# Rolling the feed-forward chunk loops of a 12-layer attention + FFN kernel into register loops, with three changes of order inside a chunk

## The chip, the cores and the metric

The kernel runs on one core of a Trainium2 chip. The metric is the device time of one execution in microseconds (us). Five engines work side by side, each from its own instruction stream: TensorE (PE, matmuls; its weight loads are shown apart as PEld), VectorE (DVE), ScalarE (ACT), GpSimd (POOL) and SyncE (SP, which here only issues DMAs). They are tied together by counting semaphores alone.

## The reference

```python
def attn(x, Wqkv, bqkv, Wproj, bproj):          # 12 layers, 16 heads, no softmax
    for i in range(12):
        qkv = x @ Wqkv[i].T + bqkv[i]
        q, k, v = split heads of qkv
        att = einsum('bhqd,bhkd->bhqk', q, k) * scale
        y = einsum('bhqk,bhkd->bhqd', att, v)
        x = y @ Wproj[i].T + bproj[i] + x
    return x

x = layernorm(x + attn(x))                      # x: (16, 256, 128) float32
gate, up = x @ wg.T, x @ wu.T                   # hidden 384, weights are integers / 127
x = layernorm(x + (silu(gate) * up) @ wd.T)
```

## The kernel before

Since the attention has no softmax, the kernel never forms the tokens' activations in the 12 layers. It keeps, for each of the 16 batches, a 128 x 128 matrix that stands for all the layers so far, and one Gram matrix of the input; each layer is a chain of small matrix products on them. This part takes the first 255 us or so and the change does not touch it.

The change is in the last stage, the feed-forward part, which runs over `CHUNKS` = 8 chunks of `CT` = 4 tiles of 128 tokens. What is done for a chunk c, by engine:

- POOL `centre` (line 329) writes the centred input of a chunk into `xc`, of which there are two slots; `rstd1_part` and the first half of `norm2` raise a 128 x 4 variance to the power -1/2 (line 366); `norm2` (line 371) then scales the finished rows into `o`, and SP (line 311) sends each finished chunk out.
- PE `z_stage` (line 910) multiplies `xc` by the batch's matrix into PSUM bank 4; `ht_stage` (line 919) transposes the normalised rows `h1` into bank 5; `gate_stage` (line 925) makes the three gate and three up products, two passes each of 128 x 512; `down_stage` (line 940) multiplies the 384 hidden rows back to 128.
- ACT `norm1` (line 465) scales z into `h1` by four small instructions; `ht_copy` (line 473) takes the upper part of the transposed rows out of PSUM; `gate` (line 477) is the silu of one gate product.
- DVE `z_part` (line 640) takes z out of PSUM; `var1_part` sums its squares; `ht_part` (line 661) makes the lower part `ht_lo`; `hid_part` (line 666) multiplies silu and up product; `y_part` (line 672) adds the residual, and a second `var_part` sums the squares of y.

In the names of the profile `sg` and `hid` are views of `xt`, `o` is `xchan`, `nu_b` is `gram`.

The chunks are software-pipelined: PE's `chunk(c)` (line 975) does the gate stage of chunk c, z of chunk c+2, the transposes of chunk c+1, and then the down stage of chunk c. The order on each engine is that in which its `chunk` function is written, and nothing else sets it. Before the change all eight calls of `chunk` are written out on every engine, with constants in every wait and address. Only PE has a second version of the eight chunks with a third pass, `chunks(True)`, whose first six chunks stand in a loop; it is taken when the lower part of the weights isn't zero. In these inputs it is zero, so that PE runs `chunks(False)` and then jumps over the other version (line 998).

`loop(eng, count)` (line 255) is a loop on one engine's instruction stream with a register as its counter and a hint for the fetch of the jump back. In it a wait for `c + 2` needs a register that holds the sum.

## Time and profile before

| | |
|---|---|
| time, median of 3 runs | 325.33 us (324.76 to 326.08) |
| the profiled execution | 325.33 us, span 323.5 us |
| PE busy | 310.8 us, 96% of the span |
| PE weight loads busy | 291.4 us, 90% |
| DVE busy | 223.2 us, 69% |
| ACT busy | 183.5 us, 57% |
| POOL busy | 95.9 us, 30% |
| mean granted TensorE clock | 0.995 of full speed |

Busy times count engine work only; register, branch and semaphore instructions are not in them. Between the span of the profile and the time of the execution lie 1.8 us. The chunks of the feed-forward part start on PE at 262.70, 269.68, 276.64, 283.60, 290.56, 297.52, 304.48 and 311.45 us, and PE's last matmul is over at about 318 us.

### The profile page before, as it was taken

What the parts mean: (1) busy time and instruction counts of PE and PEld (TensorE: products, weight loads), DVE (VectorE), ACT (ScalarE), POOL (GpSimd) and SP (SyncE); (2) the same over time, 40 slices, a digit from 0 to 9 for tenths busy, and PEclk for the clock granted to TensorE, in tenths of its full rate; (3) what the DMA queues carried; (4) which work ended last, traced back from release to release, by engine and by line L of the source; (5) the groups of instructions that cost most, each with busy time, mean ns of one, the idle gap of its engine ahead of it and who ended that gap; (6) DMA issues with size and microseconds to landing.
All of it is one profiled execution on the core that took longest, in us unless ns stands there. A gap on an engine that the chain in (4) does not pass through costs nothing.

```text
span 323.5 us, 9031 instructions
## 1 busy us (share of the span) xinstructions
PE 310.8 (96%) x3792; PEld 291.4 (90%) x3792; DVE 223.2 (69%) x638; ACT 183.5 (57%) x417; POOL 95.9 (30%) x89
## 2 busy tenths in 40 slices
PE   8999999999999999999999999999999999999993
PEld 8989899899898998989989899898998999998872
DVE  0367776775867757767577676777768568888863
ACT  2438758475583865837748477484672174445540
POOL 2014055050410603206032060230605134555432
PEclk9999999999999999999999999999999999999997
DMA  7842001020020200202002020020000000211112
GB/s 277 321 168 75 6 19 58 2 77 2 2 75 5 75 2 3 75 4 77 0 4 76 2 76 3 2 76 2 2 3 2 3 0 2 65 35 32 32 34 70
DMA packets 7594, 14.94 MB, mean 46 GB/s; under 512 B 512, under 2 KB 4736, under 8 KB 7424
## 3 DMA queue, kind: packets, MB, share of 16 engines
q1 hardware_dynamic: 6976, 13.27, 12.3%
q10 hardware_dynamic: 576, 1.06, 0.9%
q8 instruction: 32, 0.52, 0.7%
q14 instruction: 10, 0.08, 0.1%
HBM read 12.23 MB, written 2.10 MB: 44 GB/s over the span
## 4 chain that ended last, share of the span: by engine, by line
PE 92%; DVE 4%; DMA 1%; issue 1%; ACT 1%; POOLq 0%; POOL 0%
PE ps L835 14%; PE ps L782 13%; PE ps L868 13%; PE ps L734 7%; PE ps L732 7%; PE ps L733 7%; PE ps L947 6%; PE ps L801 4%; PE ps L937 3%; PE ps L936 3%; DVE s_rows L568 3%; PE ps L821 3%; PE ps L750 2%; PE ps L914 2%; PE ps L808 2%; PE ps L793 2%
## 5 line engine op out<-in xcount | busy, mean ns | idle before, releaser
L350 POOL TENSOR_TENSOR step_lo<-step,step_hi 128x512 fp32r<-128x512 f32 x44 | 54.9, 1280 | 172.3 <-ACT step_hi L431 172.3
L732 PE MATMUL ps<-state_hi,step_hi 128*128 128x258 f32 x176 | 50.7, 288 | 0.0
L835 PE MATMUL ps<-s_rows,w 32*128 32x256 f32 x768 | 44.8, 380 | 5.3 <-DVE s_rows L568 5.3
L734 PE MATMUL ps<-state_hi,step_lo 128*128 128x258 f32 x176 | 49.8, 283 | 0.0
L733 PE MATMUL ps<-state_lo,step_hi 128*128 128x258 f32 x176 | 49.6, 282 | 0.0
L835 PEld LDWEIGHTS ps<-s_rows,w 32*128 32x128 f32 x768 | 40.4, 185 | 7.2 <-ACT s_rows L425 7.2
L431 ACT CAST step_hi<-step 128x512 fp32r<-128x512 f32 x44 | 27.0, 619 | 33.7 <-DVE step L574 33.7
L782 PE MATMUL ps<-w,gram 128*128 128x128 f32 x352 | 42.8, 275 | 0.0
L782 PEld LDWEIGHTS ps<-w,gram 128*128 128x128 f32 x352 | 42.0, 192 | 0.6
L868 PE MATMUL ps<-step,gram 128*128 128x128 f32 x320 | 40.6, 281 | 0.0
L868 PEld LDWEIGHTS ps<-step,gram 128*128 128x128 f32 x320 | 37.3, 192 | 3.3 <-DVE step L574 3.3
L609 DVE TENSOR_TENSOR state_lo<-ps,state_hi 128x512 fp32r<-128x512 f32 x44 | 30.5, 692 | 12.2 <-ACT state_hi L435 10.7
L422 ACT COPY gk<-ps 128x512 f32<-128x512 f32 x48 | 28.1, 589 | 18.3 <-PE ps L782 18.3
L449 ACT COPY gram<-ps 128x256 f32<-128x256 f32 x88 | 33.0, 375 | 6.7
L574 DVE TENSOR_TENSOR step<-ps,cst 128x512 f32<-128x512 f32 x48 | 30.9, 686 | 8.3 <-PE ps L835 8.3
L621 DVE TENSOR_TENSOR state_lo<-ps,state_hi 128x256 fp32r<-128x256 f32 x88 | 36.6, 416 | 0.0
L450 ACT CAST state_hi<-ps 128x256 fp32r<-128x256 f32 x88 | 33.6, 382 | 0.0
L733 PEld LDWEIGHTS ps<-state_lo,step_hi 128*128 128x128 f32 x176 | 33.4, 190 | 0.0
L732 PEld LDWEIGHTS ps<-state_hi,step_hi 128*128 128x128 f32 x176 | 33.3, 189 | 0.0
L734 PEld LDWEIGHTS ps<-state_hi,step_lo 128*128 128x128 f32 x176 | 33.2, 189 | 0.0
L435 ACT CAST state_hi<-ps 128x512 fp32r<-128x512 f32 x44 | 25.9, 588 | 6.3 <-PE ps L868 6.3
L617 DVE TENSOR_TENSOR means<-ps,shift 128x4 f32<-128x4 f32 x88 | 14.3, 163 | 18.6 <-ACT state_hi L450 18.5
(102 smaller groups left out, 496.7 us busy)
## 6 DMA issues: line engine op xcount, KB each, us to landing
w<-weights SPq DMA_DIRECT2D x12, 592.5 KB, 3.7
xchan<-x_chan SPq DMA_DIRECT2D x1, 2048.0 KB, 10.6
out<-xchan SPq DMA_DIRECT2D x7, 256.0 KB, 2.5
xt<-x_tok ACTq DMA_DIRECT2D x4, 258.0 KB, 5.5
xt<-x_tok SPq DMA_DIRECT2D x4, 258.0 KB, 5.1
fw_int<-ffn_weights SPq DMA_DIRECT2D x1, 576.0 KB, 4.9
out<-xchan SPq DMA_DIRECT2D x2, 128.0 KB, 2.6
cst<-consts SPq DMA_DIRECT2D x1, 146.5 KB, 7.2
```

What stands on the lines that cost most here:

```text
L350: nc.gpsimd.tensor_tensor(group(step_lo, g), group(step, g), group(step_hi_f, g), ALU.subtract).then_inc(step_lo_ready, 1)
L449: nc.scalar.copy(gram[:, 2 * e:2 * e + 2, :], ps[:, two, 0:P]).then_inc(gram_ready, 1)
L450: nc.scalar.copy(state_hi[:, 2 * e:2 * e + 2, S_B:S_B + P], ps[:, two, P:2 * P]).then_inc(b_hi_ready, 1)
L574: nc.vector.tensor_tensor(group(step, g), n_banks(g // 2)[:, :, P * j:P * (j + 1)], (project if last else ident).unsqueeze(1).to_broadcast ...
L609: nc.vector.tensor_tensor(state_lo[:, GB * g:GB * (g + 1), S_H:S_H + P], products(H_BANKS[g]), state_hi_f[:, GB * g:GB * (g + 1), S_H:S_H ...
L621: nc.vector.tensor_tensor(state_lo[:, 2 * e:2 * e + 2, S_B:S_B + P], ps[:, two, P:2 * P], state_hi_f[:, 2 * e:2 * e + 2, S_B:S_B + P], ALU ...
L732: nc.tensor.matmul(dst, l_hi, r_hi, start=True, stop=False)
L733: nc.tensor.matmul(dst, l_hi, r_lo, start=False, stop=False)
L734: return nc.tensor.matmul(dst, l_lo, r_hi, start=False, stop=True)
L782: last = nc.tensor.matmul(one_product(GK_BANKS[g], b), gram_raw[:, b, 0:P] if first else gram[:, b, :], w[:, s, WK:WK + P], start=True, st ...
L835: last = nc.tensor.matmul(n_banks(h)[:, k, :], w[r, s, WQ + P * i:WQ + P * (i + 1)], s_rows[r, h, i, :], start=i == 0, stop=i == QUADS - 1)
L868: last = nc.tensor.matmul(one_product(H_BANKS[g], b), gram_raw[:, b, 0:P] if first else gram[:, b, :], step[:, b, :], start=True, stop=True)
```

## The change

It does five things.

1. SP, POOL, ACT, DVE and PE run most of their chunks in a register loop of two chunks per pass (one transfer per pass on SP). PE, DVE and ACT make three passes (chunks 0 to 5), POOL two (chunks 0 to 3), SP seven; the remaining chunks stay written out. PE's version with two passes per product, which is the one that runs, is looped too.
2. PE transposes the rows of chunk c+1 (`ht_stage`) ahead of z of chunk c+2 (`z_stage`); it was the other way round.
3. DVE follows: `ht_part(c + 1)` ahead of `z_part(c + 2)`.
4. ACT normalises chunk c+1 (`norm1`) after the first silu of chunk c instead of after the second.
5. POOL's `centre` runs three chunks ahead instead of four and stands ahead of `norm2` instead of behind it; `centre(3, 1)` ahead of the first chunk is gone, since chunk 0 now does it.

```diff
-            for c in range(CHUNKS - 1):
+            with loop(sp, CHUNKS - 1) as c:
                 sp.wait_ge(o_ready, c + 2)
...
-            def chunk(c, slot, ahead=4):
+            def chunk(c, slot, ahead=3):
 
                 if ahead >= 2:
                     pool.wait_ge(h1_ready, (c + 1) * CT + CT)
                     rstd1_part(c + 2)
+                if ahead >= 3:
+                    pool.wait_ge(z_done, c + 2)
+                    centre(c + 3, 1 - slot)
                 if ahead > 0:
                     norm2(c)
-                if ahead >= 4:
-                    pool.wait_ge(z_done, c + 3)
-                    centre(c + 4, slot)
...
-            pool.wait_ge(z_done, 2)
-            centre(3, 1)
-            for c in range(CHUNKS):
+            with loop(pool, CHUNKS // 2 - 2) as i:
+                for s in range(2):
+                    chunk(i * 2 + s, s)
+            for c in range(CHUNKS - 4, CHUNKS):
                 chunk(c, c % 2, CHUNKS - 1 - c)
...
                 gate(c, 0)
-                gate(c, 1)
                 if not last:
                     norm1(c + 1, 1 - slot)
+                gate(c, 1)
                 gate(c, 2)
...
-            for c in range(CHUNKS):
-                chunk(c, c % 2, last=c == CHUNKS - 1)
+            with loop(act, CHUNKS // 2 - 1) as i:
+                for s in range(2):
+                    chunk(i * 2 + s, s)
+            chunk(CHUNKS - 2, 0)
+            chunk(CHUNKS - 1, 1, last=True)
...
                 for j in range(HC):
                     hid_part(c, j)
-                if ahead >= 2:
-                    z_part(c + 2, c + 2, slot)
                 if ahead >= 1:
                     ht_part(c + 1)
                 if ahead >= 2:
+                    z_part(c + 2, c + 2, slot)
...
-            for c in range(CHUNKS):
-                chunk(c, c % 2, CHUNKS - 1 - c)
+            with loop(dve, CHUNKS // 2 - 1) as i:
+                for s in range(2):
+                    chunk(i * 2 + s, s)
+            chunk(CHUNKS - 2, 0, ahead=1)
+            chunk(CHUNKS - 1, 1, ahead=0)
...
+                if ahead >= 1:
+                    ht_stage(c + 1, 1 - slot)
                 if ahead >= 2:
                     pe.wait_ge(z_ready, c + 2)
                     z_stage(c + 2, c + 2, slot)
-                if ahead >= 1:
-                    ht_stage(c + 1, 1 - slot)
                 down_stage(c, last_chunk=ahead == 0)
 
             def chunks(low):
-                if low:
-                    with loop(pe, CHUNKS // 2 - 1) as i:
-                        for s in range(2):
-                            chunk(i * 2 + s, s, low)
-                for c in range(CHUNKS - 2 if low else 0, CHUNKS):
-                    chunk(c, c % 2, low, CHUNKS - 1 - c)
+                with loop(pe, CHUNKS // 2 - 1) as i:
+                    for s in range(2):
+                        chunk(i * 2 + s, s, low)
+                chunk(CHUNKS - 2, 0, low, ahead=1)
+                chunk(CHUNKS - 1, 1, low, ahead=0)
```

PE, the end of chunk 0 before the change: after the last gate product come z (L914, `ps<-a_cent,xc`), the transposes (L922, `ps<-cst,h`), and the down products (L947).

```order
L936 MATMUL ps<-ht_hi,wgu_hi 128x512 [waits silu_ready]
L937 MATMUL ps<-ht_lo,wgu_hi 128x512
L914 MATMUL ps<-a_cent,xc 128x128 [waits xc_ready,z_ready]
L914 MATMUL ps<-a_cent,xc 128x128 x3
L922 MATMUL ps<-cst,h 128x128 [waits h1_ready] x4
L947 MATMUL ps<-fw,xt 128x128 [waits hid_ready,y_ready]
```

The same place in the changed kernel, in the second chunk of the loop body, up to the first down product (now L953):

```order
L942 MATMUL ps<-ht_hi,wgu_hi 128x512 [waits silu_ready]
L943 MATMUL ps<-ht_lo,wgu_hi 128x512
L927 ISA
L928 MATMUL ps<-cst,h 128x128 [waits h1_ready]
L927 REGISTER_ALU
...
L918 REGISTER_ALU [waits z_ready]
L920 ISA [waits xc_ready]
L920 MATMUL ps<-a_cent,xc 128x128 x2
L920 ISA
L920 MATMUL ps<-a_cent,xc 128x128 x2
L951 REGISTER_ALU [waits y_ready]
L953 MATMUL ps<-fw,xt 128x128 [waits hid_ready]
```

The transposes moved ahead of z. The waits for `xc_ready`, `z_ready` and `y_ready`, which were on the matmuls, are on the sequencer's own instructions, and each transpose has a register sum ahead of it.

ACT, one chunk before the change (L479 is a silu, L470 the normalisation, L475 the copy of the transposed rows):

```order
L479 ACTIVATE xt<-ps 128x512 [waits gate_done] x2
L470 ACTIVATE h<-z,rstd 128x128 [waits y_ready,rstd1_ready]
L470 ACTIVATE h<-z,rstd 128x128 x3
L479 ACTIVATE xt<-ps 128x512 [waits gate_done]
L475 CAST ht_hi<-ps 128x512 [waits ht_done]
```

And one chunk in the changed kernel's loop (the same three as L480, L471 and L476):

```order
L480 ACTIVATE xt<-ps 128x512 [waits gate_done]
L467 REGISTER_ALU
L469 REGISTER_ALU [waits rstd1_ready]
L471 ACTIVATE h<-z,rstd 128x128 [waits y_ready]
L471 ACTIVATE h<-z,rstd 128x128 x3
L479 REGISTER_ALU
L480 ACTIVATE xt<-ps 128x512 [waits gate_done]
L479 REGISTER_ALU
L480 ACTIVATE xt<-ps 128x512 [waits gate_done]
L476 CAST ht_hi<-ps 128x512 [waits ht_done]
```

The normalisation now stands behind one silu instead of two.

## Rows read from the trace of the kernel before

**Rows 1.** The page, busy time, share of the span and instructions of an engine.
```profile
PE 310.8 (96%) x3792; PEld 291.4 (90%) x3792; DVE 223.2 (69%) x638; ACT 183.5 (57%) x417; POOL 95.9 (30%) x89
```
**Rows 2.** Busy by stage, chunks 5 and 6: window and length, PE, PEld, DVE, ACT.
```profile
297.52:304.48 6.96, 6.96 (x51) 6.34 (x50) 5.90 (x24) 3.43 (x8) 3.06 (x3) 1.00 0.13 38
304.48:311.52 7.04, 6.62 (x44) 5.49 (x42) 4.29 (x14) 3.37 (x8) 3.05 (x3) 1.00 0.14 40
```
**Rows 3.** PE, timeline of chunk 5: start us, us, engine, line, operation.
```profile
297.52 0.48 PE L936 MATMUL ps<-ht_hi,wgu_hi 128*128 128x512 f32 x1
...
300.40 1.05 PE L914 MATMUL ps<-a_cent,xc 128*128 128x128 f32 x8
301.29 0.60 PE L922 MATMUL ps<-cst,h 128*128 128x128 f32 x4
301.73 2.99 PE L947 MATMUL ps<-fw,xt 128*128 128x128 f32 x24
```
**Rows 4.** ACT, timeline of chunk 5; in brackets the idle time ahead, and its releaser.
```profile
298.27 0.60 ACT L479 ACTIVATE xt<-ps 128x512 f32<-128x512 f32 x1 [2.71 <-PE ps L937]
299.20 0.60 ACT L479 ACTIVATE xt<-ps 128x512 f32<-128x512 f32 x1 [0.34 <-PE ps L937]
299.70 1.27 ACT L470 ACTIVATE h<-z,rstd 128x128 f32<-128x128 f32 x4
300.87 0.58 ACT L479 ACTIVATE xt<-ps 128x512 f32<-128x512 f32 x1
```
**Rows 5.** DVE, timeline of chunk 5 (y's squares lie between the first two).
```profile
297.80 0.69 DVE L675 TENSOR_TENSOR y<-ps,h 128x512 f32<-128x512 f32 x1 [0.34 <-PE ps L947]
...
299.50 0.17 DVE L656 TENSOR_SCALAR ve<-var 128x4 f32<-128x4 f32 x1
299.58 1.29 DVE L669 SCALAR_TENSOR_TENSOR xt<-ps,xt 128x512 f32<-128x512 f32 x2
301.48 0.69 DVE L669 SCALAR_TENSOR_TENSOR xt<-ps,xt 128x512 f32<-128x512 f32 x1 [0.61 <-ACT xt L479]
```
**Rows 6.** POOL, timeline of chunks 4 and 5: a `centre`, and both powers.
```profile
294.87 1.04 POOL L331 TENSOR_TENSOR xc<-xchan,neg_mu 128x512 f32<-128x512 f32 x1
297.60 1.02 POOL L366 TENSOR_TENSOR rstd<-ve,minus_half 128x4 f32<-128x4 f32 x1 [1.69 <-DVE ve L656]
...
299.75 1.01 POOL L366 TENSOR_TENSOR rstd<-ve,minus_half 128x4 f32<-128x4 f32 x1 [1.14 <-DVE ve L656]
```
**Rows 7.** PE, timeline of chunk 6, which has no z: transposes, down products.
```profile
307.37 0.94 PE L922 MATMUL ps<-cst,h 128*128 128x128 f32 x4
308.15 0.62 PE L947 MATMUL ps<-fw,xt 128*128 128x128 f32 x4
309.20 2.50 PE L947 MATMUL ps<-fw,xt 128*128 128x128 f32 x20 [0.42 <-DVE xt L669]
```
**Rows 8.** ACT, timeline of chunk 6: the normalisation of chunk 7.
```profile
306.67 1.27 ACT L470 ACTIVATE h<-z,rstd 128x128 f32<-128x128 f32 x4
```
**Rows 9.** PE's sequencer: count, duration ns min/median/max, first and last start.
```profile
L998 PEldq COMPARE_BRANCH  x2: 88/2000/3911, 262.1 to 315.8; - x2
...
L769 PEldq TENSOR_LOAD <-low_flag x1: 482/482/482, 244.7 to 244.7; - x1
L769 PEldq FUSED_REGOPS  x1: 165/165/165, 245.2 to 245.2; - x1
```
**Rows 10.** Waits of PE's n stage in all layers: us in total, times, longest.
```profile
PE ps L835 <- DVE s_rows L568: 5.3, 12, 0.4
```
**Rows 11.** Timeline around 245 us: PE's first matmul after line 769.
```profile
245.79 3.52 PE L835 MATMUL ps<-s_rows,w 32*128 32x256 f32 x60 [0.44 <-DVE s_rows L568]
```
**Rows 12.** PE, timeline of the last chunk's down stage.
```profile
314.35 3.60 PE L947 MATMUL ps<-fw,xt 128*128 128x128 f32 x24
```
**Rows 13.** Timeline at chunk 0: DVE, PE's last matmul ahead, first weight load.
```profile
261.96 0.68 DVE L663 TENSOR_TENSOR ht_lo<-ps,ht_hi 128x512 fp32r<-128x512 f32 x1
...
262.56 0.39 PE L906 MATMUL ps<-cst,nu_part 128*128 128x128 f32 x2
262.69 0.19 PEld L936 LDWEIGHTS ps<-ht_hi,wgu_hi 128*128 128x128 f32 x1
```
**Rows 14.** The page, the queue that fetches PE's instructions: packets, MB.
```profile
q8 instruction: 32, 0.52, 0.7%
```

## The prediction, on record before the changed kernel ran

> **What bounds the kernel now.** I read the busy times first: PE is busy 96% of the span and its weight loads 90%, the others 69% and less [rows 1]. So only PE's time counts, and another engine or a sequencer costs something only where PE then stands still. The change touches nothing ahead of 262.7 us, so I went to the windows by chunk next. A steady chunk (0 to 5) takes 6.96 us and PE is busy in all of it; in chunk 6 PE is busy 6.62 of 7.04 us [rows 2]. The timelines of the four engines, laid side by side for chunk 5, give the deadlines. With S = 297.52, the start of the chunk on PE, z starts at S+2.88, the transposes at S+3.77, the down stage at S+4.21, the next chunk at S+6.96 [rows 3]. The one tight deadline is hidden part 2: the down stage wants it at its third product, that is its fifth of 24 records. PE takes 6.96 - 4.21 = 2.75 us for 24 records, so four take 0.46 us and the deadline is S+4.67. DVE makes that part from 301.48 to 302.17, S+4.65 [rows 5]. It just fits, because PE shows no gap. It starts that late because ACT's third silu runs only at 300.87, behind the normalisation [rows 4].
>
> The clock plays no part, 1.00 in both windows [rows 2]. The sum is made against the profiled execution, 325.33 us with a span of 323.5; it equals the median of the runs shown, and I keep the 1.8 us around the span.
>
> **Part by part: the order.** *ACT.* Today the second silu waits 0.34 us for its gate product, and then come four normalisations and the third silu [rows 4]. With the normalisation right behind the first silu that wait is filled. A silu is followed by the next work after 0.50 us (299.20 to 299.70), the normalisations take 1.17 us to the next start (299.70 to 300.87). So in chunk 5 they would start at 298.27 + 0.50 = 298.77. Their inputs: the power is over at 298.62, y at 298.49 [rows 5, 6], so both are there. Then silu 1 starts at 299.94 (0.74 later than now) and silu 2 at 300.44, 0.43 earlier. DVE's hidden part 0 ends near 300.23 (half of the x2 row); part 1 must now wait for silu 1, which ends 299.94 + 0.60 = 300.54, and part 2 follows it at once. With 0.06 us from a silu's end to DVE's start (silu 2 ends at 301.45 and DVE starts at 301.48, so 0.03 to 0.06) and 0.65 a part, part 1 runs from 300.60 and part 2 from 301.25 instead of 301.48. **Part 2 comes 0.23 us earlier.** In a steady chunk this buys nothing, since PE has no gap there; it makes slack.
>
> *PE, transposes first.* They need `h1`, which now ends at 298.77 + 1.27 = 300.04, and would start at 300.40 (S+2.88): 0.36 us to spare. They take 0.44 us and z 0.89 in either order, so the down stage stays at S+4.21. z of the chunk after next is ready 0.44 us later for DVE, at 301.73, but DVE takes it only behind part 2 and `ht_lo`, at about 302.5. `ht_lo` comes one DVE operation earlier, and the next chunk's gate stage has still more time. Nothing, in both directions.
>
> *Chunk 6.* Here no z stands between gate and transposes, and today they catch up with ACT: the normalisation runs until 306.67 + 1.27 = 307.94 [rows 8], and the four transposes started at 307.37 take 0.78 us instead of 0.44 (down starts at 308.15). After four down records PE waits 0.42 us more for hidden part 2, until 309.20 [rows 7]. With the normalisation 0.93 us earlier, as in chunk 5 (299.70 to 298.77), so over at 307.01, the transposes run at once, but the next wait, for hidden part 2, is late in its place; it ends 0.23 us earlier, at 308.97. So the 0.34 + 0.42 us of loss shrink by 0.23 only. **-0.23 us.** Chunk 7 has no ACT work moved that matters, and what follows it is unchanged: 0.
>
> *POOL.* `centre` of chunk c+2 is wanted by z of chunk c+2 in PE's chunk c. It now stands right behind the first power (297.60 to 298.62), so it ends at 298.62 + 1.04 = 299.66, S+2.14 [rows 6]. Its user now starts at S+3.31 (behind the transposes). 1.17 us to spare; if the cover were gone, each 0.1 us beyond it would cost 0.1 us in six chunks. The second power starts at 299.75, just behind it, so the output isn't moved. SP's loop only sends, seven chunks with 6.96 us each.
>
> **Part by part: the loops.** What they add is sequencer work. For PE the order lists 13 register or wait rows in the first chunk of the body and 12 in the second, and a sum and a branch at its end. The trace has three prices: 165 ns for register arithmetic, 482 for a register loaded from memory, 88 for a branch at 262.1, but 3911 ns for the other one at 315.8, a jump far ahead [rows 9]. By 165 ns, 12.5 rows are 2.1 us a chunk: nothing if hidden, 6 x 2.1 = 12.4 us if not at all. I take them as **hidden**, by this row: the load, the arithmetic and a short check at 244.7 to 245.5, some 0.68 us, stand ahead of the n stage, and PE's first matmul there came at 245.79 after waiting 0.44 us for DVE [rows 11]; the twelve such waits of all layers are 5.3 us, 0.44 each [rows 10], so this layer lost nothing by them. The sequencer had run ahead. How far: it took the branch of line 998 at 315.8, while PE's down stage ended at 314.35 + 3.60 = 317.95 [rows 9, 12]. That is **2.1 us ahead**.
>
> Some waits now hold the sequencer itself: that for `ht_lo` ahead of the gate stage, for `xc`, for `y`. What queues behind them is all of PE's further work. `ht_lo` will be there about S+5.0 (part 2 ends 301.9, one operation of 0.6 behind it), 1.9 us ahead of the next chunk; `xc` at S+2.14, 1.17 us ahead of z; y at S+0.97 [rows 5]. In each PE still has matmuls in its queue. Likewise ACT's sequencer waits for the power, ended at 298.62, 0.15 us ahead of the use: here a row of 165 ns may show, moving the normalisation some 0.1 us. I keep the 0.23 us in chunk 6, which is written out.
>
> *Entry.* At chunk 0 `ht_lo` ends at 262.64, the first weight load starts at 262.69, and PE's preceding matmuls are hardly over [rows 13]. Now the wait is passed on the sequencer and only then the weight load sent, and a jump and two setup rows stand ahead of it. Between 0 and 0.5 us (three rows of 165 ns); I take **+0.1**, since those three can run while `ht_lo` is awaited.
>
> *Sum:* 325.33 - 0.23 + 0.10 = **325.2 us**.
>
> **Back edges.** PE's, ACT's and DVE's loop jumps back twice, POOL's once. A jump to code at hand costs 88 ns, which the lead hides. What decides is whether the target is at hand.
>
> **Rivals.** *A, the jump back misses.* The 3911 ns at 315.8 are the row for it: a jump over the unused version, hidden today since PE has nothing more to do. At a back edge PE has 2.1 us of queued work, so it stands 3.91 - 2.15 = 1.8 us, twice: 3.6 us, **328.8 us**. If DVE's misses as well, its queue holds at most the squares of y, about 1.1 us; hidden part 0 would then come 3.91 - 1.1 = 2.8 us late against 0.3 of slack, 2.5 us twice, largely at the same time as PE's: up to 330.5. For it: PE's body is 2 x 48 matmul records with as many loads, near 220 instructions with the registers; 7584 PE instructions took 32 fetches of 16 KB, 237 each [rows 1, 14], so a body will mostly lie across two of them. Against it: the target is code just run, not code never fetched, and the loop carries a hint for it. It decides from 2.1 us on: a cheaper miss is hidden. Chance 0.16.
>
> The Trainium skill speaks against this change here: "Runtime: NRT & Kernel Launch", section on instruction fetch mechanics, says that a taken branch whose target isn't within the two pages at hand must fetch it first, and that kernels prefer full unrolling for it. By that rule a body across two pages still has its target at hand, unless the page fetched ahead has replaced it; the long branch at 315.8 agrees with the first half, and no run here shows a jump back.
>
> The page "Advanced Engine Details and Errata" (Control Flow Timing) gives about 108 ns for compare-and-branch; the trace has 88, and the sum is the same by either.
>
> *B, the register work shows in part.* Where a wait is passed late, the sequencer starts without a lead: five rows of 165 ns stand in the transposes and ahead of z, and they take 0.8 us where PE takes 0.44. If 0.1 to 0.5 us a chunk shows, say 0.25, six chunks give 1.5 us: **326.8 us**; up to 328. Against it: the leads of 1.2 to 2.1 us above. Chance 0.16.
>
> *C, ACT, DVE and PE gain more than the one deadline.* PE's gaps behind 262.7 are 0.34 + 0.42 in chunk 6 and 3.60 - 2.75 = 0.85 in the last down stage; all of chunk 6's gone would be 324.6. That isn't over 0.5%. Chance 0.05. Past 0.5% faster: 0.02.
>
> **How the numbers follow.** About 0.5% (1.6 us) is what a measurement of this kernel can tell from no change. Forecast 325.2 us, chance 0.63, with 324.6 to 326.0; A 0.16; B 0.16; C 0.05. B is half within 0.5% (326.96). Slower: A and half of B, 0.24. Faster: 0.02. Same: 0.74. The range takes C's 324.5 below, B whole, and reaches to A's single price, 328.8, above.
>
> **What would show it.** Right: PE's chunks every 6.96 us also from chunk 1 to 2 and 3 to 4, the edges of the body; silu 2 about 0.4 us earlier in a chunk; chunk 6's wait for hidden part 2 beginning near 307.81 and its down stage's 20 records 0.2 us earlier. A would show as branches of microseconds at chunks 2 and 4 and more fetches than chunks can use. B would show as PE idle by "issue" or chunks over 7.0 us. Wrong I would be if a wait on a sequencer empties PE's queue, which no row of before can exclude.

## The result, and the profile after

The changed kernel takes **326.64 us** (median, 325.90 to 329.58) against 325.24 us of the kernel before (324.70 to 328.79), measured in turn on the same chip: a ratio of **1.0056, 95% interval 1.0036 to 1.0077**. So it is 1.4 us slower. The forecast was 325.2 us and no change; the range of 324.5 to 328.8 held the time.

The page first: busy times as in [rows 1], then the shares of the chain that ended last, then the queue that fetches PE's instructions, as in [rows 14].

```profile
PE 312.0 (96%) x3792; PEld 291.6 (89%) x3792; DVE 227.6 (70%) x638; ACT 182.9 (56%) x417; POOL 96.6 (30%) x89
...
PE 84%; DVE 7%; issue 3%; ACT 2%; POOL 1%; DMA 1%; POOLq 0%; DVEq 0%
...
q8 instruction: 30, 0.49, 0.7%
```

DVE has the same 638 instructions and 4.4 us more work. That is the first clue: a loop adds sequencer work, which is not counted as busy, so something made DVE's own instructions longer.

The profiled execution took 327.99 us with a span of 326.2, and its chunks begin 0.4 us later than before, nearly all of it in the part that the change does not touch. So I compare lengths of chunks, not spans: of the 2.7 us between the two spans, 1.6 lie in the chunks, 0.4 ahead of them and 0.7 behind PE's last matmul. In the traces below the chunks begin between 261.9 and 264.7 us, and what follows the last matmul takes 5.2 to 6.4 us, in no order that goes with the edits. Before, each of chunks 0 to 5 took 6.96 to 6.98 us and chunk 6 6.97. After, by stage (window and length, busy us of PE, PEld, DVE, ACT, POOL, then the granted clock), chunks 1 to 4 and 6, to be set beside [rows 2]:

```profile
269.95:277.14 7.19, 7.09 (x52) 6.30 (x50) 6.65 (x24) 3.31 (x8) 4.20 (x4) 1.00 0.10 28
277.14:284.74 7.60, 7.38 (x52) 6.41 (x50) 6.82 (x25) 3.33 (x8) 4.22 (x4) 1.00 0.14 42
284.74:291.92 7.18, 7.08 (x52) 6.29 (x50) 6.82 (x25) 3.35 (x8) 4.21 (x4) 1.00 0.10 30
291.92:299.49 7.57, 7.35 (x52) 6.38 (x50) 6.82 (x25) 3.33 (x8) 4.21 (x4) 1.00 0.14 41
...
306.67:313.42 6.75, 6.46 (x43) 5.49 (x42) 4.55 (x15) 3.35 (x8) 3.05 (x3) 1.00 0.15 44
```

Chunk 0 took 6.84, chunk 5 7.18. Chunks 1 to 5 together are 36.72 us against 34.80 (+1.92), chunk 0 is 0.14 and chunk 6 0.22 shorter, and the last is 6.50 in both. The sum is +1.56; the medians differ by 1.40, and the ratio's interval allows 1.2 to 2.5. The loss has a pattern: about 0.2 us in every chunk from the second on, and 0.4 more in chunks 2 and 4. The clock is 1.00 throughout and plays no part.

PE itself does the same things. Only its down stage, the last row of a chunk, is longer (PE, timeline of chunks 0 to 3: start, us, engine, line, operation; compare 2.99 in [rows 3]):

```profile
267.36 2.84 PE L953 MATMUL ps<-fw,xt 128*128 128x128 f32 x24
...
274.17 3.21 PE L953 MATMUL ps<-fw,xt 128*128 128x128 f32 x24
...
281.35 3.63 PE L953 MATMUL ps<-fw,xt 128*128 128x128 f32 x24
...
288.95 3.21 PE L953 MATMUL ps<-fw,xt 128*128 128x128 f32 x24
```

2.84 us is what the stage's 24 records (twelve products) take when nothing holds them. The table of waits after 255 us names who does (us in total, times, longest): the loads of line 953 wait for `hid`, which the profile calls `xt`.

```profile
PEld ps L953 <- DVE xt L673: 3.3, 11, 0.4
```

So DVE's hidden parts come late. The timeline of DVE in chunk 2 shows the cause, and a second one (in brackets the idle time ahead):

```profile
277.42 0.69 DVE L679 TENSOR_TENSOR y<-ps,h 128x512 f32<-128x512 f32 x1
278.14 0.29 DVE L656 CUSTOM_DVE_ANT_0 sq<-y 128x128 f32<-128x128 f32 x1
...
278.36 0.29 DVE L656 CUSTOM_DVE_ANT_0 sq<-y 128x128 f32<-128x128 f32 x1
...
278.57 1.12 DVE L656 CUSTOM_DVE_ANT_0 sq<-y 128x128 f32<-128x128 f32 x1
...
279.63 0.28 DVE L656 CUSTOM_DVE_ANT_0 sq<-y 128x128 f32<-128x128 f32 x1
...
279.95 0.17 DVE L660 TENSOR_SCALAR ve<-var 128x4 f32<-128x4 f32 x1
280.54 1.89 DVE L673 SCALAR_TENSOR_TENSOR xt<-ps,xt 128x512 f32<-128x512 f32 x3 [0.42 <-ACT xt L480]
```

One of the four squares of y takes 1.12 us instead of 0.29. What stands beside it is on POOL (timeline, the same chunk):

```profile
277.38 1.01 POOL L366 TENSOR_TENSOR rstd<-ve,minus_half 128x4 f32<-128x4 f32 x1 [2.12 <-DVE ve L660]
278.36 1.19 POOL L331 TENSOR_TENSOR xc<-xchan,neg_mu 128x512 f32 x1
```

`centre` runs from 278.36 to 279.55, and the long square, sent at 278.57, ends at 279.69. In [rows 5, 6] the POOL instruction beside y's squares was the power, which reads 128 x 4 elements, and `centre` stood at 294.87, away from them.

The second cause is the 0.42 us ahead of the hidden parts. The bracket names ACT, but ACT's silu 0 had been done for two microseconds (ACT, same chunk):

```profile
277.89 0.60 ACT L480 ACTIVATE xt<-ps 128x512 f32<-128x512 f32 x1 [3.83 <-PE ps L943]
278.50 1.28 ACT L471 ACTIVATE h<-z,rstd 128x128 f32<-128x128 f32 x4
279.69 1.06 ACT L480 ACTIVATE xt<-ps 128x512 f32<-128x512 f32 x2
```

Chunk 2 is where DVE's loop has jumped back. Its sequencer's rows in 279 to 281 us (duration ns minimum, median, maximum; first and last start) show when:

```profile
L709 DVEq COMPARE_BRANCH  x1: 90/90/90, 280.0 to 280.0; - x1
L709 DVEq BRANCH_PREFETCH_HINT  x1: 39/39/39, 280.3 to 280.3; - x1
L709 DVEq FUSED_REGOPS  x1: 74/74/74, 280.4 to 280.4; - x1
```

The jump was taken at 280.0, once `ve` (279.95) had been started, not microseconds ahead of it. In the next chunk, in the middle of the loop's body, the same two instructions follow each other without a gap (DVE, timeline):

```profile
287.55 0.17 DVE L660 TENSOR_SCALAR ve<-var 128x4 f32<-128x4 f32 x1
287.72 1.89 DVE L673 SCALAR_TENSOR_TENSOR xt<-ps,xt 128x512 f32<-128x512 f32 x3
```

PE's jumps back are these, again with the unused version's jump of line 1003, as in [rows 9]:

```profile
L993 PEldq COMPARE_BRANCH  x3: 80/236/258, 275.3 to 304.9; - x3
...
L1003 PEldq COMPARE_BRANCH  x2: 92/2106/4120, 262.4 to 317.8; - x2
```

Two causes, then, for 1.9 us, neither of which the prediction had. The experiments were to say which part of the change brings which, and what each costs.

### The profile page after: what moved, and what is told of

Same layout as the page of the kernel before. It is cut to its first block, busy times and chain, and to the rows that moved or that the text cites. A ratio compares the mean times of both kernels' runs of the same rounds, so it can differ in the third digit from the quotient of the medians.

```text
span 326.2 us, 9259 instructions
## 1 busy us (share of the span) xinstructions
PE 312.0 (96%) x3792; PEld 291.6 (89%) x3792; DVE 227.6 (70%) x638; ACT 182.9 (56%) x417; POOL 96.6 (30%) x89
## 4 chain that ended last, share of the span: by engine, by line
PE 84%; DVE 7%; issue 3%; ACT 2%; POOL 1%; DMA 1%; POOLq 0%; DVEq 0%
PE ps L841 14%; PE ps L788 13%; PE ps L874 13%; PE ps L740 7%; PE ps L738 6%; PE ps L739 6%; PE ps L807 4%; PE ps L953 3%; PE ps L827 3%; PE ps L756 2%; DVE s_rows L572 2%; DVE xt L673 2%; PE ps L942 2%; PE ps L943 2%; PE ps L814 2%
## 5 line engine op out<-in xcount | busy, mean ns | idle before, releaser
L613 DVE TENSOR_TENSOR state_lo<-ps,state_hi 128x512 fp32r<-128x512 f32 x44 | 30.4, 692 | 12.2 <-ACT state_hi L436 10.7
L480 ACT ACTIVATE xt<-ps 128x512 f32<-128x512 f32 x24 | 13.4, 587 | 27.5 <-PE ps L943 27.5
```

What stands on the lines that cost most here:

```text
L613: nc.vector.tensor_tensor(state_lo[:, GB * g:GB * (g + 1), S_H:S_H + P], products(H_BANKS[g]), state_hi_f[:, GB * g:GB * (g + 1), S_H:S_H ...
```

## The experiments

Each group was timed in turns with the kernel before on one chip (its median there was 325.25 to 325.5 us). Letters in the expectations name theories; they are not the rivals A to C of the prediction:

- C: `centre` collides with DVE's squares. L: the loops cost the time by themselves. I: they do once PE waits for DVE. F: they are free as long as PE alone is the bound.
- N: the kernel before had nothing to win in a steady chunk. A: all that the orders win is the earlier third hidden part (in the expectations "hidden part 2", since they count from 0).
- D: the deadline of the third hidden part turns DVE's lateness into PE's.
- H: a square is held until the POOL instruction that it meets ends. S: it is held, or slowed, for as much in all however `centre` is cut.
- J: DVE's jump back costs the 0.4 us of every second chunk. G: DVE's order of z and `ht_lo` sets the 7.09 us.

Chunk lengths are between the starts of the first gate product on PE.

**The loops alone.** `e4_loops_old_order` is the kernel before with part 1 of the change and nothing else, on all five engines:

```diff
-            for c in range(CHUNKS):
-                chunk(c, c % 2, CHUNKS - 1 - c)
+            with loop(dve, CHUNKS // 2 - 1) as i:
+                for s in range(2):
+                    chunk(i * 2 + s, s)
+            chunk(CHUNKS - 2, 0, ahead=1)
+            chunk(CHUNKS - 1, 1, ahead=0)
```

> The kernel before with the loops alone, POOL, ACT, DVE and PE in the old order. Theory C: 325.3 us, chunks of 6.96 us. Theory L: 326.6 us.

325.29 us, ratio 0.9991 (0.9964 to 1.0018), every chunk 6.95 to 6.97. **The loops cost nothing by themselves.** But DVE's gap at the jump back is there (DVE, chunk 2; `ve` is over at 278.90):

```profile
278.73 0.17 DVE L662 TENSOR_SCALAR ve<-var 128x4 f32<-128x4 f32 x1
279.32 1.29 DVE L675 SCALAR_TENSOR_TENSOR xt<-ps,xt 128x512 f32<-128x512 f32 x2 [0.42 <-ACT xt L482]
```

It is hidden, because in the old order the third hidden part waits for ACT's third silu anyway, which runs there from 280.10 to 280.68.

**The new order alone.** `e3_unrolled_new_order` is the changed kernel with all chunks written out again, that is parts 2 to 5 of the change; the edit is the one above, backwards, on every engine.

> The changed kernel without its loops: all four changes of order, every chunk written out. Theory C: 326.4 us, as the changed kernel within 0.3. Theory L: 325.0 us.

325.97 us, 1.0008 (0.9969 to 1.0047); chunks 6.83, five times 7.08 or 7.09, and 6.74. The squares are held as in the changed kernel, and chunks 2 and 4 are like the others. So the 0.4 us of every second chunk needs the loops, the 0.13 us of all of them does not. C was right on the squares, but not in its forecast that this version would be as slow as the changed kernel; each theory had one of the two causes.

**POOL's order alone, and all but POOL's.** `e2_before_centre_first` puts only part 5 into the kernel before. `e5_unrolled_order_but_pool` does parts 2 to 4 (PE, DVE and ACT) and leaves POOL and the loops as before; `e6_loops_order_but_pool` is the same with the loops.

```diff
                     rstd1_part(c + 2)
+                if ahead >= 3:
+                    pool.wait_ge(z_done, c + 2)
+                    centre(c + 3, 1 - slot)
                 if ahead > 0:
                     norm2(c)
-                if ahead >= 4:
-                    pool.wait_ge(z_done, c + 3)
-                    centre(c + 4, slot)
```

> The kernel before, all written out, with POOL's change alone: centre three chunks ahead, in front of norm2. Theory C: one square of y of about 1.1 us in each of chunks 1 to 4 or 5, and since ACT's order is the old one DVE has only 0.61 + 0.35 us idle: 0.2 to 0.5 us a chunk, 326.3 to 327.5 us. Theory L: no loops, so 325.2 us.

> The changes of order on PE, DVE and ACT alone, written out, POOL in the old order (centre behind norm2, four ahead). Theory C (POOL's centre holds a square of y on DVE, and hidden part 2 is then late for PE): no long square, and since hidden part 2 comes 0.2 us earlier than before, chunks of 6.83 us, as chunk 0 of the changed kernel shows; with chunk 6 0.2 us shorter 324.1 us. Theory N (before had no gap to win in a steady chunk): chunks of 6.96 us, 325.0 us.

> The changed kernel, loops and all, with POOL's order and its centre four ahead as before. Theory C: without the long square DVE has room for its jump back (some 0.4 us from the last instruction of a pass to the first of the next), chunks of 6.83 us, 324.2 us. Theory I (the loops cost by themselves once PE waits for DVE): every second chunk 0.3 to 0.4 us longer, chunks of 6.83 and 7.2 us in turn, 325.0 us.

| | median us | ratio to before | steady chunk | chunk 6 |
|---|---|---|---|---|
| e2, POOL's order alone | 326.2 | 1.0021 (0.9989 to 1.0053) | 7.09 | 6.95 |
| e5, PE, DVE, ACT orders | 324.24 | 0.9971 (0.9940 to 1.0001) | 6.81 | 6.62 |
| e6, the same and loops | 324.43 | 0.9968 (0.9940 to 0.9997) | 6.81 | 6.63 |

The totals of e2 and e5 reach 1 with their intervals; the chunks of their traces are plain. (C had put e2 at 0.2 to 0.5 us a chunk, and it is 0.13.) POOL's new place makes a chunk 7.09 us long under the old orders as under the new ones, from 6.96 and from 6.81. And without it the loops cost nothing even with the new orders: DVE's gap is hidden again. In e2 the held square is the second of four (DVE, timeline):

```profile
284.67 1.12 DVE L650 CUSTOM_DVE_ANT_0 sq<-y 128x128 f32<-128x128 f32 x1
```

**Where the gain of e5 is from.** `e11_before_act_order` moves only ACT's normalisation (part 4):

```diff
                 gate(c, 0)
-                gate(c, 1)
                 if not last:
                     norm1(c + 1, 1 - slot)
+                gate(c, 1)
                 gate(c, 2)
```

> The kernel before with ACT's change of order alone. Theory A (what the orders gave is hidden part 2 0.2 us earlier, and nothing else): chunks of 6.81 to 6.83 us, 324.2 us. If PE's transposes ahead of z had their share: between 6.83 and 6.96, 324.7 us or more.

324.25 us, 0.9968 (0.9956 to 0.9981), chunks 6.80 to 6.82 and 6.63: all of e5's gain. The down stage is at its floor (PE, and ACT with its second and third silu in one row, timelines):

```profile
286.62 2.84 PE L947 MATMUL ps<-fw,xt 128*128 128x128 f32 x24
```
```profile
284.82 1.06 ACT L479 ACTIVATE xt<-ps 128x512 f32<-128x512 f32 x2
```

Against 2.99 in [rows 3]: each steady chunk of the kernel before had waited 0.15 us for the third hidden part, while PE was busy by the profile in all of it. The orders of PE and DVE bring nothing more.

**How the held square works.** `e9_e3_centre_in_halves` is e3 with `centre` as two instructions of 256 columns:

```diff
-                nc.gpsimd.tensor_tensor(
-                    xc[:, slot, :].rearrange("p (b t) -> p b t", b=2),
...
+                for b in range(2):
+                    last = nc.gpsimd.tensor_tensor(
+                        xc[:, slot, T * b:T * (b + 1)].unsqueeze(1),
...
+                last.then_inc(xc_ready, 1)
```

> The written-out kernel with all four new orders (chunks of 7.09 us, third square of y 1.12 us), with each centre made by two POOL instructions of 256 columns instead of one of 512. Theory H (DVE's square is held until the POOL instruction that it met ends): it gets in between the halves, some 0.55 us long instead of 1.12; with 0.5 us less on DVE the chunks are 6.83 to 6.9 us and the time 324.5 us. Theory S (POOL holds on until its queue of reads is through, or DVE is slowed by shared bandwidth): the squares together stay 0.8 us longer, chunks of 7.09 us, 325.6 us.

325.57 us, 1.0019 (1.0004 to 1.0034), chunks still 7.07 to 7.08. DVE, and then POOL:

```profile
285.56 0.69 DVE L652 CUSTOM_DVE_ANT_0 sq<-y 128x128 f32<-128x128 f32 x1
...
286.18 0.69 DVE L652 CUSTOM_DVE_ANT_0 sq<-y 128x128 f32<-128x128 f32 x1
```
```profile
285.41 1.31 POOL L332 TENSOR_TENSOR xc<-xchan,neg_mu 128x256 f32<-128x256 f32 x2
```

The mechanism of H held, its number did not; the number that came is that of S. A square waits for the end of the POOL instruction that it meets, 0.69 us now instead of 1.12; but the second half meets the next square, and 2 x 0.40 is as much as 1 x 0.83. That each long square ends some 0.14 us after one of the halves, and that the square sent at 285.34 still took 0.29 beside the first half, speaks for being held by one instruction and against a general slowing by shared bandwidth; no run tests the two apart further.

**The 0.4 us of every second chunk.** `e13_after_dve_written_out` is the changed kernel with DVE's chunks written out; PE, ACT, POOL and SP keep their loops.

```diff
-            with loop(dve, CHUNKS // 2 - 1) as i:
-                for s in range(2):
-                    chunk(i * 2 + s, s)
+            for c in range(CHUNKS - 2):
+                chunk(c, c % 2)
```

> The changed kernel with DVE's eight chunks written out; PE, ACT, POOL and SP keep their loops. Theory J (the extra 0.4 us of every second chunk is DVE's jump back, met when DVE is late from the held square): all of chunks 1 to 5 take 7.1 to 7.2 us, as in the version written out everywhere, and the time is 0.5 to 0.9 us below the changed kernel's 326.6. If another engine's loop does it (PE's branch took up to 258 ns, ACT's and POOL's wait on the sequencer), 7.57 stays in every second chunk.

325.45 us, 0.9993 (0.9967 to 1.0019), chunks 6.84, five times 7.09, and 6.75, together 1.27 us shorter than the changed kernel's, where J had said 0.5 to 0.9. J's cause was right: DVE's loop alone is the difference, and the other four loops stay free although DVE is late here. On DVE in chunk 2 the hidden parts now follow at once:

```profile
279.07 0.17 DVE L660 TENSOR_SCALAR ve<-var 128x4 f32<-128x4 f32 x1
279.15 1.89 DVE L673 SCALAR_TENSOR_TENSOR xt<-ps,xt 128x512 f32<-128x512 f32 x3
```

From `ve` to the hidden parts it is 0.08 us here, 0.17 in the changed kernel's middle chunks, and 0.59 and 0.56 at its two jumps. The steps of 0.09, 0.51 and 0.48 are those from 7.09 to 7.18, 7.60 and 7.57 us.

**DVE's order.** `e14_e3_dve_order_back` is e3 with z ahead of `ht_lo` again on DVE.

```diff
+                if ahead >= 2:
+                    z_part(c + 2, c + 2, slot)
                 if ahead >= 1:
                     ht_part(c + 1)
                 if ahead >= 2:
-                    z_part(c + 2, c + 2, slot)
```

> The version written out with all new orders, with DVE's z ahead of ht_lo again. In the new order the squares of z wait for z just written, 0.22 us of gap where before ht_lo lay between. Theory G (this gap keeps DVE at its limit beside the held square): chunks shorter than 7.09, about 6.95, and 325.0 us. If hidden part 2's path through PE alone sets the pace: 7.09 us still, 325.8 us.

325.17 us, 0.9989 (0.9961 to 1.0017), chunks again 7.09, chunk 6 6.63. G was wrong for the steady chunks (it is right for chunk 6 alone, 6.63 against 6.74 in e3): DVE has idle time of 0.35 us ahead of y there, where e3 has 0.11, and what it saves only makes it wait longer (DVE, timeline):

```profile
283.70 0.69 DVE L673 TENSOR_TENSOR y<-ps,h 128x512 f32<-128x512 f32 x1 [0.35 <-PE ps L945]
```

So 7.09 us is a circle through both engines, not DVE's own work: y waits for the down stage, and the next down stage for the hidden parts behind y's squares.

**`centre` behind `norm2`.** `e1_after_centre_last` keeps the three chunks ahead but puts `centre` behind `norm2`:

```diff
                     rstd1_part(c + 2)
+                if ahead > 0:
+                    norm2(c)
                 if ahead >= 3:
                     pool.wait_ge(z_done, c + 2)
                     centre(c + 3, 1 - slot)
-                if ahead > 0:
-                    norm2(c)
```

> The changed kernel with POOL's centre (three chunks ahead) put back behind norm2; loops and all other orders stay. Theory C (collision): in the changed kernel centre starts 0.2 us into the third square of y on DVE, which then takes 1.12 us instead of 0.29; behind norm2 it runs beside operations that read PSUM. Expects squares of 0.29 us, chunks of 6.96 us and 325.1 us. Theory L (loops): the register rows on the sequencers cost the 0.4 us a chunk; expects chunks of 7.2 to 7.6 us still and 326.6 us.

**343.06 us**, 1.0515 (1.0462 to 1.0568), a clear miss of mine. The two POOL rows ahead of it, and the matmuls that wait (POOL, then PE, chunk 1, which takes 9.2 us):

```profile
274.38 1.04 POOL L375 TENSOR_TENSOR xchan<-y,rstd 128x512 f32 x1 [0.19 <-POOL rstd L366]
275.38 1.04 POOL L331 TENSOR_TENSOR xc<-xchan,neg_mu 128x512 f32 x1
```
```profile
276.57 1.15 PE L920 MATMUL ps<-a_cent,xc 128*128 x8 [2.14 <-POOL xc L331]
```

With three chunks ahead, what `centre` writes is wanted by z in the same chunk of PE, and behind the second power and `norm2` it comes at 276.42. PE stands 2.0 to 2.1 us in each of chunks 1 to 5. In chunks 2, 3 and 5, of 10.7 to 10.8 us, its granted clock falls too, to a mean of 0.84; behind the wait in chunk 3 (296.60 to 298.47) it is 0.50, the 1.2 GHz level. Chunks 1 and 4, with the same wait, have 1.00 (2.4 GHz) and take 9.2 us. The run's time says nothing on the two causes, but its trace does: all 28 squares of y take 0.28 to 0.29 us, as C had said of this place, and DVE's 0.42 us at the jump is still there. And it shows that `centre`'s new place belongs to its new distance.

**A down stage that asks for the last hidden part last.** The tight deadline in the steady chunks is the third hidden part, wanted by the stage's third product. `e12_act_order_down_by_part` is e11 with the down stage running over the parts outside and the tiles inside:

```diff
-                for t in range(CT):
-                    for j in range(HC):
-                        if t == 0:
-                            pe.wait_ge(hid_ready, n * HC + (HC + j + 1))
...
-                                                wd[:, j, :], start=j == 0, stop=j == HC - 1)
+                order = [(j, t) for j in range(HC - 1) for t in range(CT)] + [(HC - 1, t) for t in range(CT)]
+                for j, t in order:
+                    if t == 0:
+                        pe.wait_ge(hid_ready, n * HC + (HC + j + 1))
...
+                                            wd[:, j, :], start=j == 0 and (t == 0 or last_chunk and t == CT // 2),
+                                            stop=j == HC - 1 and (t == CT - 1 or last_chunk and t == CT // 2 - 1))
```

The start flag stands on a bank's first product only. `e8_e5_down_by_part` and `e10_e6_down_by_part` do the same to e5 and e6, and `e7_after_down_by_part` to the changed kernel.

> The changed kernel with one more edit: the down stage takes hidden parts 0 and 1 for all four tiles first and part 2 last, so that part 2 is wanted at the 17th record instead of the 5th, 1.3 us later. Theory D (the deadline of hidden part 2 is what turns DVE's lateness into PE's): PE's waits shrink, but DVE's own work in a chunk, with the long square and the gaps around it, is near 7.1 us and sets the pace; chunks of 7.0 to 7.2 us instead of 7.18 and 7.57, and 0.3 us less each in chunks 6 and 7: 325.0 us. If the deadline doesn't matter: 326.6 us.

> The orders of PE, DVE and ACT of the change, written out, POOL as before, and the down stage by hidden part. Theory D: chunks 0 to 5 of 6.8 us, chunk 6 without its wait for hidden part 2 (0.4 us less), the last chunk's down stage 0.3 to 0.6 us shorter: 323.4 us, below both kernels. If the deadline doesn't matter: as the version without that edit.

> Loops, PE, DVE and ACT in the new order, POOL in the old one, and the down stage by hidden part: the best version so far, with loops. DVE has 0.3 to 0.5 us of slack a chunk, as much as its jump back takes. Theory F (loops are free as long as no engine but PE is the bound): chunks of 6.81 us and 322.6 us. Otherwise every second chunk is longer by up to 0.4 us, 323.5 us.

> The kernel before with ACT's change of order and the down stage by hidden part, nothing else. Theory A: as the version with all three orders, chunks of 6.81 us and 322.5 us. If the transposes ahead of z matter: 323 us or more.

| | median us | ratio to before | steady chunk | chunk 6 |
|---|---|---|---|---|
| e7, changed kernel | 325.13 | 0.9985 (0.9960 to 1.0010) | 6.81 to 7.34 | 6.32 |
| e8, e5 | **322.50** | 0.9914 (0.9882 to 0.9946) | 6.81 to 6.83 | 5.92 |
| e10, e6 (with loops) | 323.09 | 0.9928 (0.9913 to 0.9944) | 6.81 to 6.83 | 5.92 |
| e12, e11 | 322.96 | 0.9929 (0.9913 to 0.9944) | 6.80 to 6.82 | 5.92 |

The gain is at the end, where no z stands ahead of the down stage. The last one took 3.60 us in [rows 12]; e12's two last on PE:

```profile
306.92 2.84 PE L947 MATMUL ps<-fw,xt 128*128 128x128 f32 x24
...
312.42 2.92 PE L947 MATMUL ps<-fw,xt 128*128 128x128 f32 x24
```

That is 0.7 us in chunk 6 and 0.7 in chunk 7; from e6 to e10 the medians differ by 1.34, from e11 to e12 by 1.29. D had put e8 at 323.4 us, 0.9 too high, and F had put e10 at 322.6, 0.5 too low. e12's 322.96 lies between A's 322.5 and the 323 or more that would have given the transposes a part; its chunks, the same as e8's, decide for A. In e7 this doesn't free the steady chunks. With the third part's deadline gone, the path through DVE is still longer than PE's 6.81: DVE's rows there stand one behind the other, with the square of 1.12 us and, at a jump, the 0.42 us in them (DVE, timeline: the hidden parts of chunk 2 and a square in chunk 3):

```profile
281.93 1.89 DVE L673 SCALAR_TENSOR_TENSOR xt<-ps,xt 128x512 f32<-128x512 f32 x3 [0.42 <-ACT xt L480]
...
287.45 1.12 DVE L656 CUSTOM_DVE_ANT_0 sq<-y 128x128 f32<-128x128 f32 x1
```

e8, e10 and e12 beat both kernels; e12 does it with the fewest edits, and e10 with the loops kept. Their intervals overlap, so I don't rank them.

## Why the prediction was wrong, and where it was right

**The step that failed is POOL's**, with two others behind it: the worth of ACT's order, put at 0 in a steady chunk, and DVE's loop, taken as hidden. The part on POOL weighed `centre`'s new place against one deadline, z of the same chunk, and against POOL's own queue. Both hold: no z waits for `xc` in the changed kernel, and what the second power waits for is DVE's `ve`, not `centre` (0.66 us idle ahead of it at 280.20, though it starts 3.1 us into the chunk now, 2.2 before). It never asked what DVE does in those microseconds. By its own numbers `centre` was to run from 298.62 to 299.66, and y's squares lie from y's end at 298.49 to `ve` at 299.50 [rows 5, 6]. The price is 0.83 us on one square, of which 0.28 a chunk is left on the path (7.09 against 6.81), +1.4 us in five chunks, and 0.12 in chunk 6 (6.74 in e3, 6.62 in e5). The trace of before had a row for it, which I did not read: ahead of the first chunk a square met a `centre` and took 1.09 us, the one long square of all 60 there (timeline of the kernel before):

```profile
258.82 1.04 POOL L331 TENSOR_TENSOR xc<-xchan,neg_mu 128x512 f32<-128x512 f32 x1
...
258.91 1.09 DVE L652 CUSTOM_DVE_ANT_0 sq<-z 128x128 f32<-128x128 f32 x1
```

The Trainium skill has this rule, in "SBUF — State Buffer", section "Who interferes with whom": DVE and GpSimd share one pair of SBUF ports under an exclusive lock, a DVE instruction with two SBUF inputs contends with a GpSimd instruction that reads SBUF, and the order of issue decides who is blocked. The trace agrees: 1.12 us against 0.29, ending 0.14 us after `centre`, and 0.69 when `centre` was halved; `centre`, sent while a square ran, took 1.19 us against 1.04. The squares' two inputs are both y, in SBUF; the hidden parts, with one input in PSUM, kept their length beside `norm2` (1.89 us for three). Not every POOL instruction that reads SBUF holds a square, though: in e3 one runs inside the power, 128 x 4 elements, at its usual length (POOL, then DVE, timelines):

```profile
278.54 1.01 POOL L366 TENSOR_TENSOR rstd<-ve,minus_half 128x4 f32<-128x4 f32 x1 [2.21 <-DVE ve L654]
```
```profile
279.23 0.29 DVE L650 CUSTOM_DVE_ANT_0 sq<-y 128x128 f32<-128x128 f32 x1
```

The rule would have given the rival that spoke against this change; none of the prediction's three used it.

**"In a steady chunk this buys nothing, since PE has no gap there" was wrong.** ACT's new order was sized right in the third silu's time, but its worth was put at 0 in six chunks. The profile's busy PE was taken as proof of no wait. The down stage took 2.99 us and needs 2.84; a matmul that stands with its operands late is shown as busy. e11 has -0.15 us a chunk, -0.9 in six. My S+4.67 for the deadline was worked out from those same 2.75 us between starts, that is, with the wait inside it; in e11 the 24 records take 2.60 us between starts.

**The loops, on PE, ACT, POOL and SP: right.** Registers and jumps are hidden by work queued ahead (e4, e6, e13). The price of 165 ns was far too high: the register rows of the loop bodies take 32 to 84 ns, on PE at most 60. Rival A did not come true: PE's jumps back took 80 to 258 ns and its instructions were fetched in 30 packets against 32.

The Trainium skill's advice to unroll fully, in "Runtime: NRT & Kernel Launch", section on instruction fetch mechanics, was worth nothing for the fetches here: no jump back shows a miss. That a branch to a target outside the pages at hand must first fetch it agrees with the far jump's 4120 ns; whether the targets of the jumps back lay inside them is not shown, only that those jumps took 258 ns at most.

**The loop on DVE: wrong.** The lead of 2.1 us was read on PE and carried to DVE, whose queue I had holding all the squares. DVE's sequencer reached its jump at 280.0, when `ve` (279.95) had been started, so with no lead at all. The price is some 0.50 us at a jump (0.51 and 0.48) and 0.09 us in a chunk without one. It shows only where DVE is late, which `centre` had seen to; in e4 and e6 it is there and costs nothing. The two parts of the change cost more together than apart: by the chunks of the traces, orders -1.3 (e5), POOL's place +1.5 (e5 to e3), the loops 0 without it (e6) and +1.3 with it (e13 to the changed kernel). Rival B named 326.8 us, close to the time, and its reason ("a wait is passed late, without a lead") was in part this one, but on PE and in all chunks, where nothing of it showed.

**Smaller terms.** Chunk 6 was to gain 0.23 us and gained 0.22, but that is luck. ACT's order alone gains 0.34 (e11, 6.63 against 6.97), and `centre`'s place and DVE's new order together take 0.11 back: 6.74 in e3, but 6.62 without the one (e5) and 6.63 without the other (e14). In e3 DVE is so late with the squares of z that the power for this chunk's normalisation is over only at 307.90, and the normalisation starts at 307.93. The wait that is left in the changed kernel stands behind two records, so it is for the second hidden part, not the third (PE, timeline):

```profile
310.00 0.39 PE L953 MATMUL ps<-fw,xt 128*128 128x128 f32 x2
310.57 3.09 PE L953 MATMUL ps<-fw,xt 128*128 128x128 f32 x22 [0.19 <-DVE xt L673]
```

The entry was to cost 0.1: from start to start the first gate product follows the last product ahead of it by 0.23 us, by 0.14 before, so +0.09. The transposes ahead of z bring nothing in either direction, as said.

The account by the runs for chunks 1 to 5: ACT's order 5 x -0.15, `centre` 5 x +0.28, DVE's loop 3 x 0.09 + 2 x 0.50, together +1.92, which is what the windows show. The three prices were read from these chunk lengths or from other versions' of the same kind, so the sum shows that nothing is left over, and is no independent test. That the loop on DVE costs this is shown by e13. That the 0.42 us is the sequencer's own time behind an instruction that waits, rather than something else at the jump, is only read from the order of its rows; no run took it apart further, nor the 0.09 us.

## What to carry to other kernels

Before moving an instruction to another engine's idle time, lay the timelines of all engines side by side at its new place, and look in the trace for the longest of each kind of instruction, not only the mean: a 1.09 beside 0.29 is worth a look at what ran beside it. A matmul stage that is busy all the time still waits if the same number of products takes less elsewhere in the trace; compare stages with their shortest. And a lead measured on one engine's sequencer is not another's: ask at each jump what stands ahead of it in the queue.

## What the hardware showed that I had not expected

- A fused square-and-sum on DVE, both inputs the same tile, was held for the rest of `centre`, a POOL instruction of 128 x 512 that reads SBUF, 0.29 us becoming 1.12; halving `centre` gives two of 0.69 and saves nothing. `centre` is longer as well, 1.19 us against 1.04. The power of 128 x 4 beside a square did nothing to it.
- At its jumps back DVE's sequencer had no lead over `ve`, the instruction ahead, which waits for the squares: they left DVE idle for 0.42 and 0.39 us, while PE's and ACT's jumps in the same program cost nothing.
- Register rows of 32 to 84 ns against the 165 that one row of before had; jumps back of 55 to 90 ns on DVE and 80 to 258 on PE.
- The first square of z starts 0.22 us later when z is the instruction just ahead of it: in e3 the first square of z starts at 284.34, z being 283.52 to 284.20, which is 0.82 from start to start, where before the change `ht_lo` stood between and the square followed that in 0.59 (295.73 to 296.32). The first square of y follows y in 0.73. What makes the difference was not tested.
